# A fused two-layer kernel: routed experts computed for every token, or only for their own tokens in sorted tiles

## What is computed

```python
scores = sigmoid(xf @ gate_w.T + gate_b)
top_scores, top_idx = top_k(scores, 2)
top_scores = top_scores / (top_scores.sum(-1, keepdims=True) + 1e-06)
comb = (one_hot(top_idx, 8) * top_scores[..., None]).sum(1)
hdn = gelu(einsum('th,ehf->etf', xf, w1) + b1)      # 8 experts, h = 128, f = 512
y = einsum('etf,efh->eth', hdn, w2) + b2
routed = einsum('te,eth->th', comb, y)
shared = (gelu(xf @ sw1 + sb1) @ sw2 + sb2) * 0.1
```

## Time and profile before

| | |
|---|---|
| time, median of 3 runs (range) | 862.85 us (862.37 to 865.46) |
| the profiled execution: its own time | 867.54 us |
| the profiled execution: span from first to last instruction | 865.8 us |
| mean granted TensorE clock | 0.92 of 2.4 GHz |
| PE busy | 772.1 us (89%) |
| DVE, ACT, POOL busy | 458.9, 334.6, 291.2 us |
| bytes moved by transfers | 26.61 MB |

### The profile page before, as it was taken

How to read it: one execution, slowest core, us unless ns; L and a number is a source line. 1 busy time by engine, 2 the same in 40 slices (tenths; PEclk the granted TensorE clock), 3 DMA queues, 4 the chain that set the end, 5 groups by cost and what they waited for, 6 DMA issues and landing times.

```text
span 865.8 us, 12588 instructions
## 1 busy us (share of the span) xinstructions
PE 772.1 (89%) x4993; PEld 440.7 (51%) x4993; DVE 458.9 (53%) x837; ACT 334.6 (39%) x507; POOL 291.2 (34%) x205
## 2 busy tenths in 40 slices
PE   5889999999889997899997989999789999978957
PEld 3333434434566465366554636556445664653533
DVE  0451304050347564769648477953765973648570
ACT  4523434433245453253534325443334452532410
POOL 0540000000002244366335445642543652443550
PEclk9799999999779997899998889999899999988986
DMA  7500000000111100000001010111000000100000
GB/s 298 238 13 13 0 0 12 0 12 0 61 61 28 41 10 14 12 14 25 17 10 38 14 26 1 25 25 37 14 5 22 14 26 13 38 14 20 7 1 13
DMA packets 22488, 26.61 MB, mean 31 GB/s; under 512 B 1291, under 2 KB 18339, under 8 KB 21796
## 3 DMA queue, kind: packets, MB, share of 16 engines
q1 hardware_dynamic: 22436, 25.88, 9.5%
HBM read 23.71 MB, written 2.16 MB: 30 GB/s over the span
## 4 chain that ended last, share of the span: by engine, by line
PE 64%; DVE 27%; issue 3%; POOL 2%; ACT 2%; DMA 1%; DVEq 0%; POOLq 0%; SPq 0%; ACTq 0%
PE ps L642 10%; PE ps L653 9%; PE ps L552 7%; PE ps L544 5%; PE ps L602 4%; PE ps L674 4%; PE ps L716 4%; PE ps L704 3%; PE ps L626 3%; PE ps L666 2%; DVE x_sb L1069 2%; PE ps L535 2%; DVE small L1085 2%; DVE l L1136 2%; PE ps L536 2%
## 5 line engine op out<-in xcount | busy, mean ns | idle before, releaser
L653 PE MATMUL ps<-work,mw 128*128 128x512 f32 x288 | 142.4, 641 | 23.0 <-DVE mtmp L1104 23.0
L892 ACT ACTIVATE work<-ps,cols 128x512 f32<-128x512 f32 x144 | 98.6, 688 | 114.1 <-PE ps L642 102.8
L642 PE MATMUL ps<-xn,mw 128*128 128x512 f32 x256 | 119.3, 610 | 0.0
L653 PEld LDWEIGHTS ps<-work,mw 128*128 128x128 f32 x288 | 58.5, 206 | 96.5 <-issue 68.3
L466 POOL TENSOR_TENSOR small<-small 128x8 f32<-128x8 f32 x32 | 54.5, 1718 | 122.7 <-DVE small L1078 122.7
L642 PEld LDWEIGHTS ps<-xn,mw 128*128 128x128 f32 x256 | 48.8, 197 | 55.4 <-issue 50.1
L1077 DVE TENSOR_REDUCE small<-sq 128x8 f32<-128x512 f32 x32 | 21.8, 680 | 90.1 <-ACT sq L880 90.1
L449 POOL CAST xb_s<-xn 128x512 fp32r<-128x512 f32 x4 | 2.4, 612 | 199.1 <-DVE xn L969 199.1
L457 POOL TENSOR_TENSOR small<-small 128x8 f32<-128x8 f32 x32 | 55.5, 1751 | 18.8 <-DVE small L1086 17.6
L704 PE MATMUL ps<-l 64*64 64x64 f32 x1024 | 36.2, 244 | 26.8 <-DVE sq L1092 26.8
L552 PE MATMUL ps<-work,l 128*128 128x512 f32 x128 | 57.4, 607 | 2.7 <-ACT work L828 2.7
...
## 6 DMA issues: line engine op xcount, KB each, us to landing
comb_bc<-comb_dram SPq DMA_DIRECT2D x32, 256.0 KB, 4.7
...
l<-in_h SPq DMA_DIRECT2D x2, 1024.0 KB, 7.7
...
x_sb<-in_xT SPq DMA_DIRECT2D x1, 1024.0 KB, 5.0
x_dram<-x_sb SPq DMA_DIRECT2D x4, 256.0 KB, 2.4
l<-x_dram SPq DMA_DIRECT2D x4, 256.0 KB, 3.3
out<-l SPq DMA_DIRECT2D x4, 256.0 KB, 2.4
```

What stands on the lines that cost most here:

```text
L642: mm = pe.matmul(to, mw1[:, e - NSPLIT, f * P:(f + 1) * P], xn[:, i * NB:(i + 1) * NB], start=True, stop=True)
L653: mm = pe.matmul(bank(7), mw2[:, e * KC + f], hid[:, e % 2, f], start=(f == 0), stop=(f == KC - 1))
L892: act.activation(hid[:, e % 2, f], take("up", i, (e, f)), ACT.Gelu, bias=col("b1", e * KC + f)).then_inc(r_act, 1)
```

## The change

The eight routed experts are no longer computed for all tokens. Each of the 4096 (token, expert) pairs gets a slot in an array of 5120 slots, sorted by expert, each expert's region starting at a multiple of 128: 40 tiles of 128 slots, each of one expert only (4 tiles are a "quad"). The shared expert stays as it was in size: its first product is made in three float32r products per matmul as before, its second is moved into `project_out`.

- DVE computes the slots: after the combine weights a mask, a running sum, and (from two small matmuls of PE) the rank of each pair, in 11 further small operations before `key_variances(0, 0)`; after `gradients(0, 0)`, and ahead of `weights(0, 0)`, the expert of each tile and the tile's biases (`tile_tables`, 10 operations).
- PE transposes x to token-major (16 transposes, after the gate), ACT copies it out, and POOL scatters the rows to DRAM by 32 indirect transfers of 128 rows of 512 bytes, 8 in each chunk of block 0, at three places of POOL's order (3, 2 and 3 of them).
- Blocks 1 and 2 compute five quads each. Per quad: SP loads 512 slots, PE transposes them (4), ACT copies them out; per tile: 4 matmuls `tiles_up` of 128 columns, 4 gelus of 128x128 on ACT, 4 matmuls `tiles_down`; per quad ACT copies bank 7 out and SP stores it to DRAM.
- The weights of a tile come from DRAM per tile: SP waits until tile k - 3 is through `tiles_down`, reads the expert's number from SBUF into a register and issues two transfers of 256 KB, into one of three buffers.
- In block 3 POOL gathers the results by 32 indirect transfers, ACT scales them, and PE turns and adds the two of each token (`routed_out`, 8 matmuls of 128x128 per block of tokens); DVE adds them to the output (`add_routed`).
- `mix`, the broadcasts (32 transfers of 256 KB) and the two loads of all experts' weights (4.35 MB) are gone. An SP transfer fills the 2.6 MB of slots with zeros at the start. `project_out(i - 1)` moves from ahead of `keys_through(i, 1)` to behind it, ahead of `project_queries(i)`, and has 4 matmuls more (128x512). `x` is loaded back once, 1 MB, and the output is stored in the last block.

Chunk 0 of blocks 1 and 2 holds the first two quads (the last two `tiles_down` of the second stand behind `updates(i, 0)`), chunk 2 the third and fourth in the same way, chunk 3 the fifth. Blocks 0 and 3 have no tiles.

```diff
+            def slots_in(n):
+                if n >= 2:
+                    sp.wait_ge(r_act, taken_no["qt", n - 2, 0])
+                sp.dma_start(xg[:, n % 2], xs_dram[n * 4 * P:(n + 1) * 4 * P].rearrange("(t p) d -> p t d", p=P))\
+                    .then_inc(xg_ld[n % 2], 16)
+
+            def weights_in(k):
+                if k >= 3:
+                    sp.wait_ge(d_pe, k - 2)
+                e = sp.value_load(tile_e[0:1, k:k + 1], min_val=0, max_val=EXP - 1)
+                sp.dma_start(wtile[:, k % 3, 0], a["mw1"][:, bass.ds(e, 1), :]).then_inc(w_ld[k % 3], 16)
+                sp.dma_start(wtile[:, k % 3, 1].rearrange("p (k d) -> p k d", d=D),
+                             a["mw2"].rearrange("p (e k) d -> p e k d", k=KC)[:, bass.ds(e, 1)]).then_inc(w_ld[k % 3], 16)
+
+            comb_of(0)
+            sp.wait_ge(b_bias, 1)
+            sp.wait_ge(x_st, NBLK * 16)
+            sp.dma_start(acc[:, :], x_dram).then_inc(x_ld, 16)
+            sp.wait_ge(b_tile, 1)
+            sp.wait_ge(x_sc, 2 * NT * 16)
+            slots_in(0)
+            for k in range(3):
+                weights_in(k)
+            slots_in(1)
+            for k in range(4 * QUADS):
+                n = k // 4
+                if k + 3 < 4 * QUADS:
+                    weights_in(k + 3)
+                if k % 4 == 0 and n + 2 < QUADS:
+                    slots_in(n + 2)
+                if k % 4 == 3:
+                    sp.wait_ge(y_ev, n + 1)
+                    sp.dma_start(ys_dram[n * 4 * P:(n + 1) * 4 * P].rearrange("(t p) d -> p t d", p=P),
+                                 ybuf[:, n % 2]).then_inc(y_st[n % 2], 16)
+                    if n in (1, 6):
+                        comb_of(1 if n == 1 else 2)
...
+            def scatter_rows(count):
+                for _ in range(count):
+                    s, j = divmod(moved["out"], NT)
+                    moved["out"] += 1
+                    if s == 0 and j == 0:
+                        pool.wait_ge(z_st, 16)
+                        pool.wait_ge(b_pos, 1)
+                        pool.wait_ge(r_act, taken_no["x", 0, 3])
+                    pool.indirect_dma_start(xs_dram, bass.IndirectOffsetOnAxis(
+                        ap=pos[:, s * NT + j:s * NT + j + 1], axis=0), xtok[:, j, :], None).then_inc(x_sc, 16)
...
                     pool.tensor_tensor(gx[:, h], gx[:, h], ttok[:, c % 2, h], ALU.add).then_inc(z_gx.sem, 1)
+                    rows(i, 3)
                     pool.wait_ge(z_s2.sem, z_s2.at(i, c + 1))
                     pool.tensor_tensor(qd(sq[:, h]), qd(xh[:, h]), over_d(small[:, 48:56]),
                                        ALU.mult).then_inc(z_u.sem, 1)
                     if c or i:
                         query_deviations(*((i, c - 1) if c else (i - 1, NCH - 1)))
                         pool.wait_ge(q_pe.sem, q_pe.at(i, 2 * c) if c else q_pe.at(i - 1, 2 * NCH))
+                    rows(i, 2)
                     for p in range(2):
...
+            def tiles_up(n, *which):
+                for t in which:
+                    k = 4 * n + t
+                    pe.wait_ge(r_act, taken_no["qt", n, 0])
+                    pe.wait_ge(w_ld[k % 3], 32 * (k // 3 + 1))
+                    to = free("mu", n, t)
+                    for f in range(KC):
+                        mm = pe.matmul(to[:, f * P:(f + 1) * P], wtile[:, k % 3, 0, f * P:(f + 1) * P],
+                                       xgT[:, n % 2, t * P:(t + 1) * P], start=True, stop=True)
+                    mm.then_inc(r_pe, 1)
+
+            def tiles_down(n, *which):
+                for t in which:
+                    k = 4 * n + t
+                    if t == 0:
+                        bank7_free("y", n)
+                    pe.wait_ge(r_act, taken_no["mu", n, t])
+                    for f in range(KC):
+                        mm = pe.matmul(bank(7)[:, t * P:(t + 1) * P], hidt[:, k % 2, f],
+                                       wtile[:, k % 3, 1, f * P:(f + 1) * P], start=(f == 0), stop=(f == KC - 1))
+                    mm.then_inc(d_pe, 1)
...
             def project_out(i):
-                pe.wait_ge(m_mul.sem, m_mul.at(i + 1, 3) if i + 1 < NBLK else m_mul.at(i, NE))
+                bank7_free("out", i)
                 pe.wait_ge(b_cld.sem, b_cld.at(i, 16))
+                pe.wait_ge(r_act, taken_no["su", i, KC - 1])
+                pe.wait_ge(ld_m, 16)
                 pe.matmul(bank(7), wqo[:, :], xn[:, i * NB:(i + 1) * NB], start=True, stop=False)
                 pe.matmul(bank(7), mb2[:, :], combT[:, :], start=False, stop=False)
+                for f in range(KC):
+                    pe.matmul(bank(7), sw2[:, f], hid[:, f], start=False, stop=False)
                 pe.wait_ge(r_act, taken_no["v", i, (NCH - 1, 1)])
                 for q in range(NQ):
                     mm = pe.matmul(bank(7), wo[:, q], xqT[:, q], start=False, stop=(q == NQ - 1))
                 mm.then_inc(t_out.sem, 1)
...
                 turn_keys(i, 0)
                 project_targets(i, 1)
-                up(i, 0)
+                if i == 0:
+                    shared_up(0)
+                if qs:
+                    slots_turned(qs[0])
+                    tiles_up(qs[0], 0, 1)
                 if i:
                     turn_queries(i - 1, 2)
-                up(i, 1)
-                down(i, 0)
+                if qs:
+                    tiles_down(qs[0], 0)
+                    tiles_up(qs[0], 2)
+                    tiles_down(qs[0], 1)
+                    tiles_up(qs[0], 3)
+                    tiles_down(qs[0], 2, 3)
                 if i:
                     queries_through(i - 1, NCH - 1)
-                up(i, 2)
-                down(i, 1)
-                up(i, 3)
-                down(i, 2)
+                if qs:
+                    slots_turned(qs[1])
+                    tiles_up(qs[1], 0, 1)
+                    tiles_down(qs[1], 0)
+                    tiles_up(qs[1], 2)
+                    tiles_down(qs[1], 1)
+                    tiles_up(qs[1], 3)
                 updates(i, 0)
 
                 if i:
                     turn_queries(i - 1, 3)
+                if qs:
+                    tiles_down(qs[1], 2, 3)
+                keys_through(i, 1)
+                if i:
                     project_out(i - 1)
-                keys_through(i, 1)
                 project_queries(i)
                 project_targets(i, 2)
                 turn_keys(i, 1)
                 queries_through(i, 0)
-                up(i, 4)
-                down(i, 3)
                 updates(i, 1)
 
                 turn_queries(i, 0)
-                up(i, 5)
+                if i:
+                    shared_up(i)
                 keys_through(i, 2)
+                if qs:
+                    slots_turned(qs[2])
+                    tiles_up(qs[2], 0, 1)
                 queries_through(i, 1)
                 turn_keys(i, 2)
                 project_targets(i, 3)
-                down(i, 4)
-                up(i, 6)
-                down(i, 5)
-                up(i, 7)
-                down(i, 6)
+                if qs:
+                    tiles_down(qs[2], 0)
+                    tiles_up(qs[2], 2)
+                    tiles_down(qs[2], 1)
+                    tiles_up(qs[2], 3)
+                    tiles_down(qs[2], 2, 3)
+                    slots_turned(qs[3])
+                    tiles_up(qs[3], 0, 1)
+                    tiles_down(qs[3], 0)
+                    tiles_up(qs[3], 2)
+                    tiles_down(qs[3], 1)
+                    tiles_up(qs[3], 3)
+                if i == NBLK - 1:
...
+            def tile_gelus(n, *which):
+                for t in which:
+                    k = 4 * n + t
+                    src = take("mu", n, t)
+                    if k == 0:
+                        act.wait_ge(b_bias, 1)
+                    if k >= 2:
+                        act.wait_ge(d_pe, k - 1)
                     for f in range(KC):
-                        act.activation(hid[:, e % 2, f], take("up", i, (e, f)), ACT.Gelu,
-                                       bias=col("b1", e * KC + f)).then_inc(r_act, 1)
+                        ins = act.activation(hidt[:, k % 2, f], src[:, f * P:(f + 1) * P], ACT.Gelu,
+                                             bias=b1t[:, k * KC + f:k * KC + f + 1])
+                    ins.then_inc(r_act, 1)
+
+            def tiles_back(n):
+                act.wait_ge(d_pe, 4 * n + 4)
+                if n >= 2:
+                    act.wait_ge(y_st[n % 2], n // 2 * 16)
+                act.activation(ybuf[:, n % 2].rearrange("p t d -> p (t d)"), bank(7), ACT.Copy).then_inc(y_ev, 1)
...
             def finish(i):
                 dve.wait_ge(t_out.sem, t_out.at(i, 1))
-                stt(macc[i % 2][:, :], bank(7), be_wo[:, 0:1], macc[i % 2][:, :], ALU.add,
-                    ALU.add).then_inc(t_res.sem, 1)
+                dve.wait_ge(x_ld, 16)
+                o = by_batch(acc[:, i * NB:(i + 1) * NB])
```

(10 more changed lines are left out.)

442 lines of the change are left out of this document (306 added, 136 removed).

## The result

The changed kernel takes **884.93 us** (median of 4 runs, 884.63 to 886.60), the kernel before beside it 862.74 us (4 runs, 862.37 to 865.46): ratio 1.0254, 95% interval 1.0230 to 1.0279. Slower by 22 us; 874.0 had been forecast. The profiled execution took 885.09 us, its span is 883.3 us, and its mean granted clock 0.842 (before 0.92).

The account below looks back on a forecast made before the run. PE, waiting for DVE in places, was taken to bound the kernel. Step times summed to a span of 874.0, plus 3 for POOL 877, 11 over 865.8; the same 11 on the median gave 874 us, range 846 to 914.

Parts of the forecast that it names:

- U3: Start of `updates` of a block's fourth chunk; predicted at 391.0 us in block 0 and 835.9 in block 3.
- step 0: From U3 of the block before to U0 of this block; predicted 40.5, 31.5 and 21.5 us in blocks 1 to 3.
- the tail: From U3 of block 3 to the end: 32.1 us plus 6 for four more matmuls, `routed_out` and its hand-overs.
- L: Time from a tile's `tiles_down` to usable weights in its freed buffer; taken as 5.0 us, bounds 4.0 and 7.
- Steps 2 and 3: Second to third and third to fourth `updates` of a block; predicted 40.9 and 37.0 us in blocks 1 and 2.
- A half: One tile's `up` or `down` on PE, 4 matmuls; taken as 0.93 us, with 1.86 at 1.2 GHz as far end.
- Step 1: First to second `updates` of a block; predicted 43.6 us in blocks 1 and 2, 44.8 in block 3.
- U0: Start of `updates` of a block's first chunk; predicted at 431.5 us in block 1 and 584.5 in block 2.
- Rival 1: In the tile blocks weights come in time, L under about 3.7: 27 us back, about 847; chance 0.24.
- Rival 2: POOL becomes the bound at 2.5 us per indirect transfer: about 6 us a chunk in seven chunks, about 915; chance 0.10.
- `tile_tables` 5.8 us: DVE's tile table operations ahead of `weights(0, 0)` in block 0, about 5.8 us by columns.
- Slots: 6 us at the start of block 1: Added to step 0 of block 1: slots and weights can't load until POOL's last scatters have landed; 6 us.

## Why the prediction was right, and where its terms were off

The direction, the mechanism and the place of the loss were as forecast: 55 us of PE go from each block, and steps 1 and 3 and the way into block 1 take them back. Point by point:

- **The span: 883.3 instead of 877.** By the table, U3 of block 0 came 2.7 us later than predicted, step 0 of block 1 cost 1.5 more, block 1's steps 2.1 more, step 0 of block 2 1.8 more, block 2's steps 0.6 less, block 3 2.2 more, the tail 0.3 less: 9.3 us over the 874.0 of the sum, of which the 3 us for POOL cover a part. The other 4.6 us of the 10.9 on the median come from the last line of the sum: it put the same 11 us on the median of the kernel before, though that kernel's profiled execution was 4.7 us over its median, while the one after stood on its own (885.09 and 884.93).
- **L = 5.0 (bounds 4.0 and 7).** It was 4.44: register and wake-up 0.91 where I took 1.0, and 3.53 from the first issue to `tiles_up` (414.45 to 417.98) where I took 4.0. The term that was off is the second 256 KB: with 3.1 us from issue to landing (2.8 taken) and its issue 0.43 us behind the first, the two make up the 3.53, and nothing like 0.7 comes on top. Steps 2 and 3 came out 0.5 to 1.1 us shorter than predicted, as a shorter L would have it. The Trainium skill's 600 ns, by which L would have been 4.6, came nearer in the sum, but by luck: its term stands for the stretch to the first issue, which measured 0.91.
- **A half = 0.93.** Measured from start to start 0.90 and 0.89 (412.64, 413.54): right. It lies between the 0.86 by columns and the 0.93 of the transposes, so it doesn't tell which of the two sets it. PE busy fell by 110 us where the sum said some 140; stretches at the lower clock are part of that (`updates` alone 45.5 us against 36.2), the rest wasn't taken apart.
- **Step 1 = 43.6 (44.8 in block 3).** 47.5, 44.4 and 46.3. Keys to `gradients` took 23.1 us (443.24 to 466.34), predicted 23.0. What was missing in block 1 is ahead of it: two downs and the turning ran at half clock (3.42 us for 16 records), so that the keys came at U0 + 7.6 instead of + 4.7. What failed here is that the clock's price was put at zero for this step: "the trace shows it for a long pause only". Between 436 and 444 the granted clock was 0.57 (the window below). A pause for weights of 2.52 us (434.55) lies in front of it, and with the read ahead one of 1.94 us (430.42) was enough for `updates` at half speed. It isn't the length alone: behind 2.62 us (508.92) and 2.56 us (591.36) PE ran at full speed, and step 1 of block 2 is 44.4 us here but 47.4 and 47.5 in the kernels with the tables late and with the read ahead.
- **Rival 1: 27 us, at L under 3.7.** The price was 31, and steps without waits were foreseen as 37.1, 33.3 and 26.8: 36.7, 32.8 and 25.1. Its condition was too wide, as L = 3.74 showed, and its own steps give 24.4 and not 27 (3.8, 3.7 and 4.7, twice). 3.2 us of the price are the clock in step 1 of block 1, where no weights are awaited.
- **Rival 2, POOL.** Where they follow each other, an indirect transfer of 128 rows comes every 1.26 us (predicted 1.2), so it fell as a bound (a single one took 2.39 us, in the kernel with the tables late); but two more of them ahead of `keys_through` cost 7.7 us in step 2 of block 0, through PE.
- **`tile_tables` 5.8 us.** 9.6 us, beside POOL. The second keys still came near their forecast (301.58, predicted 300.9), so what stands ahead of the tables was priced too dear by about 3 us: two errors of opposite sign.
- **Slots: 6 us at the start of block 1.** PE waited 4.6 us for `xg` at 404.86, and with early scatters step 0 was 9.1 us shorter: right, if a little small.

The window in step 1 of block 1, and POOL's transfers beside the keys of block 0's step 2, both of the changed kernel:

```profile
436.00:444.00 8.00, 8.00 (x85) 7.77 (x82) 1.38 (x2) 3.57 (x9) 2.50 (x2) 0.57 0.07 16
...
336.67 0.98 POOL L541 DMA_INDIRECT xs_dram<-wtile,pos  x1 [0.17 <-issue]
337.96 0.96 POOL L541 DMA_INDIRECT xs_dram<-wtile,pos  x1 [0.30 <-issue]
```

The prediction's errors partly cancelled, so part of its closeness is luck: L too long by 0.6 us (by the slope seen above some 12 us of time, though steps 2 and 3 show only 3.2 of it), the clock and the tables too cheap. The range of 846 to 914 was needed for that, and so was the chance of 0.24 for a gain: by the same slope the break-even lay 1.0 us of L away, and with 0.7 taken off the kernel was still 6 us slower than before.
